# Product rows added by VectorE through a PSUM bank, and the Toeplitz kernel split once, in a gated long-convolution and MoE kernel

## The chip, the cores and the metric

The kernel runs on one core of one Trainium2 chip. A core has TensorE (PE), VectorE (DVE), ScalarE (ACT), GpSimd (POOL) and SyncE (SP, which here only issues DMAs). The metric is the device time of one execution in microseconds (us). Three runs of the kernel before took 830.1, 830.31 and 832.09 us, the median is 830.31.

## The reference

x is (8, 256, 512), the context c the same shape. All is float32.

```python
kv  = einsum('bhil,bhjl->bijhl', c, c)          # 32 heads of 8 channels, L = 512
y   = causal convolution of kv with ssm_kernel[h] along l      # by FFT
out = einsum('bijhl,bhil->bjhl', y + kv * D[h], layernorm(x))
x   = x + tanh(g_xattn) * out
t   = layernorm(x)
x   = x + tanh(g_ffn) * (sum of top-2 of 16 SwiGLU experts, weighted + 2 shared SwiGLU blocks)(t)
```

Per head there are 8 x 8 products kv, of which 36 are distinct, since k and v are the same context. D is added to the kernel's first tap.

## The kernel before, in words

The program has two stages. The first (convolution, residual, layernorm, gate logits, storing of t) works on 16 tiles of 128 rows, one tile a turn. A tile is two heads, each with 8 channels and 8 batches. The second is the expert feed-forward with routing; the change doesn't touch its code.

A turn t of stage one, by engine. Each engine runs its own list of instructions in order and waits on semaphores:

- **SP** issues the loads of tile t+2 (context cx, Toeplitz rows toep, x in xt and xr, a slice `stage` of the shared weights) and the stores of tile t-1 (x2, t, tT), in the order of its `turn`. toep is read from a small table kpad in HBM, whose rows overlap, so that partition p holds the kernel shifted by p.
- **POOL**: `form` multiplies the context into kv, 36 x 64 = 2304 elements a partition, for tile t+1 (L367, L371); then `split_shared` (L1270), `split_toep` (L380) and its part of `split_kv` (L1276). kv has one buffer: `form` of the next tile waits until both parts of kv_lo are made.
- **ACT**: the square root for the second layernorm of tile t-1 (L543), shared_hi (L594), toep_hi (L581), kv_hi (L588), the normalised t (L557), the same for x of tile t+1 (L539, L549), copies of PE's transposes (L567, L568, L574).
- The **hi and lo** parts: PE multiplies in a rounded float32 form, so each operand is a rounded hi and a rest lo = value - hi, and each product is three matmuls (hi hi, hi lo, lo hi).
- **PE**: the turn has four blocks lb = 0..3 of 128 positions. `conv` of block lb has 6(lb+1) matmuls of 288 columns (L1135) in a pair of PSUM banks, for two heads; 60 a turn. `sum_rows` adds seven rows of products with seven accumulating transposes (L1145); it stands behind the next block's `conv`. `gate` (L1115, 8 rows), `turn_t` and `turn_q` (L1095, 4 each) make up the rest.
- **DVE**: `products` of each block multiplies y in PSUM by q, per head with three instructions (L750 256 elements, L753 192, L756 64) into nine rows of 128 in the SBUF tile prod, then one instruction adds two rows to two others (L760, 256 elements, all in SBUF). Between the blocks stand `residual` (L721, behind block 0, with the statistics L697, L699, L700), `scale_x2` and `stats_x` (behind block 1), `scale_x` and DVE's part of kv_lo (L766, 1280 elements, behind block 2).

Engines alternate between two buffers of nearly everything (cx, toep, kv_hi, kv_lo, q, prod, the two pairs of PSUM banks). Turns 3 to 14 are a hardware loop.

Of the kernel before, what the change touches and what calls it, by code (L numbers as in the profile page):

```python
# [146 lines left out]
def program(nc, x, ctx_ext, conv_rows, conv_d, gates, gate_w, weights, out):  # L147
    ctx = ExitStack()
    with ctx:
# [12 lines left out]
        kpad = nc.dram_tensor("kpad", (HEADS, 640), F32, kind="Internal").ap()  # L162
# [3 lines left out]
        toeplitz = bass.AP(kpad.tensor, 0, [[2 * 640, TILES], [1, P], [640, 2], [1, L]])  # L166
# [30 lines left out]
        toep = sb2("toep", [P, 2 * L], F32, one)  # L197
# [76 lines left out]
        toeph_ok, toepl_ok = sem("toeph_ok"), sem("toepl_ok")  # L274
        conv_ok, prod_ok, summed = sem("conv_ok"), sem("prod_ok"), sem("summed")
# [100 lines left out]
        def split_toep(eng, t):  # L376

            p = t.odd
            wait(eng, toeph_ok, t + 1)
            eng.tensor_tensor(toep_lo[p][:], toep[p][:], toep_hi[p][:].bitcast(F32), ALU.subtract).then_inc(toepl_ok, 1)  # L380
# [20 lines left out]
        def _(sp):  # L401
# [79 lines left out]
            sp.wait_ge(toepl_ok, TILES)  # L481
# [49 lines left out]
        def _(act):  # L531
# [44 lines left out]
            def split_toep_hi(t):  # L576

                p = t.odd
                wait(act, conv_ok, (t - 1) * 8)
                wait(act, toep_in[p], (t.half() + 1) * 16)  # L580
                act.activation(toep_hi[p][:], toep[p][:], ACT.Copy).then_inc(toeph_ok, 1)  # L581

# [103 lines left out]
        def _(dve):  # L686
# [5 lines left out]
            dve.tensor_tensor(krow[:, P - 1:P], krow[:, P - 1:P], drow[:], ALU.add).then_inc(kpad_ok, 1)  # L692

# [40 lines left out]
            def products(t, lb):  # L734
# [5 lines left out]
                for h in range(2):  # L740
                    y = ps_conv[par][h][:]
# [37 lines left out]
            split_kv(At(0))  # L779
            split_toep(dve, At(0))  # L780
# [3 lines left out]
            def turn(t):  # L784
# [305 lines left out]
        def _(pe):  # L1090
# [12 lines left out]
            def turn_t(t):  # L1103
                wait(pe, tT_ok, t)
                wait(pe, t_ok, t + 1)
                turn_rows(t1[t.odd], ps_t, t_turned)

            def gate(t):
# [5 lines left out]
                for c in range(BLOCKS):  # L1114
                    last = pe.matmul(ps_gate[:, 0:EXPERTS], tT[t.odd][:, c * P:(c + 1) * P],  # L1115
# [3 lines left out]
            def conv(t, lb):  # L1119
# [3 lines left out]
                for h in range(2):  # L1123
                    if h == 0:
                        if lb == 0:
                            wait(pe, toepl_ok, t + 1)
                            wait(pe, kvl_ok, t + 1)
                            wait(pe, kvl2_ok, t + 1)
                        wait(pe, prod_ok, (t * 4 + lb - 1) * PROD_STEPS)
                    for mb in range(lb + 1):  # L1130
# [3 lines left out]
                        for m, (w, z) in enumerate(((toep_hi, kv_hi), (toep_hi, kv_lo), (toep_lo, kv_hi))):  # L1134
                            mm = pe.matmul(ps_conv[lb % 2][h][:, 0:n], w[p][:, k:k + P], z[p][:, o:o + n],  # L1135
# [3 lines left out]
            def sum_rows(t, lb):  # L1139
# [3 lines left out]
                wait(pe, prod_ok, (t * 4 + lb + 1) * PROD_STEPS)  # L1143
                for r in ROWS_LEFT:
                    mm = pe.matmul(ps_o[:, lb * P:(lb + 1) * P], prod[lb % 2][:, r * P:(r + 1) * P], ident[:],  # L1145
                                   is_transpose=True, start=(r == ROWS_LEFT[0]), stop=(r == ROWS_LEFT[-1]))
# [112 lines left out]
        def _(pool):  # L1259
# [21 lines left out]
            def turn(t):  # L1281
# [118 lines left out]
```

## Time and profile before

| what | value |
|---|---|
| median of the runs | 830.31 us |
| the profiled execution | 832.62 us |
| its span, first to last instruction | 830.8 us |
| mean granted TensorE clock | 0.97 of full |
| stage one, about | 0 to 290 us |
| PE busy | 756.1 us, 91% |
| DVE busy | 657.3 us, 79% |
| ACT busy | 444.6 us, 54% |
| POOL busy | 382.4 us, 46% |
| L760, the add of product rows | x64, 108.3 us |
| L766, DVE's part of kv_lo | x16 |

Busy time is the sum of the records of an engine, and a share over the whole span mixes two stages with different limits. For this change only stage one matters, where a turn starts with the first L750 of the tile's block 0; the turn lengths are differences of such starts.

### The profile page before, as it was taken

The numbers are of one execution on the slowest core, as the hardware profiler recorded it, in microseconds if no ns is written. First come the engines' busy times: TensorE is split into PE (matmuls) and PEld (weight loads), VectorE is DVE, ScalarE is ACT, GpSimd is POOL, SyncE is SP. The second block draws the span as 40 slices with busy tenths as digits, with TensorE's granted clock in tenths as the row PEclk, the third lists the DMA queues.
The fourth block names the chain that finished last, engine by engine and source line by source line (L and its number), as shares of the span: only waits on it lengthen the run. The fifth ranks groups of instructions, "written<-read, shape, count | busy, mean of one in ns | idle before, by whom it ended". The sixth has DMA issues, their size and how long they took to land.

```text
span 830.8 us, 15761 instructions
## 1 busy us (share of the span) xinstructions
PE 756.1 (91%) x4730; PEld 708.6 (85%) x4730; DVE 657.3 (79%) x1167; ACT 444.6 (54%) x594; POOL 382.4 (46%) x206
## 2 busy tenths in 40 slices
PE   3888887787889999999999999989999999999994
PEld 3887787787888889999999999979989989899993
DVE  7999999999999854684258958866986885896891
ACT  5333344343343233221258958766876875895882
POOL 5767657667567001451123443534444344554242
PEclk9999899999889999999999999999999999999997
DMA  6334544334442213121724668767656665443200
GB/s 231 123 122 137 169 153 135 133 121 158 159 141 77 90 64 52 32 45 26 266 51 134 168 168 236 190 197 180 183 168 149 196 170 162 102 80 63 53 14 0
DMA packets 43027, 105.86 MB, mean 127 GB/s; under 512 B 7121, under 2 KB 7121, under 8 KB 42961
## 3 DMA queue, kind: packets, MB, share of 16 engines
q1 hardware_dynamic: 30128, 80.15, 28.4%
q0 software_dynamic: 12832, 24.93, 15.6%
q8 instruction: 30, 0.49, 0.2%
q14 instruction: 37, 0.30, 0.1%
HBM read 148.87 MB, written 29.18 MB: 214 GB/s over the span
## 4 chain that ended last, share of the span: by engine, by line
PE 58%; DVE 24%; issue 7%; DMA 4%; ACT 2%; SPq 1%; ACTq 1%; DVEq 0%; POOL 0%; POOLq 0%
PE bank L1198 29%; PE bank L1223 16%; DVE prod L760 9%; PE bank L1135 5%; DVE prod L750 3%; DVE prod L753 3%; PE bank L1145 3%; PE bank L1206 3%; DMA raw<-in_weights 2%; PE bank L1095 2%; DVE st L697 2%; DMA out<-ys,slot_info 2%; DVE prod L756 1%; DVE kv_lo L766 1%; ACT w_hi L663 1%
## 5 line engine op out<-in xcount | busy, mean ns | idle before, releaser
L1068 DVE TENSOR_TENSOR w_lo<-raw,w_hi 128x1408 fp32r<-128x1408 f32 x94 | 148.8, 1621 | 45.9 <-ACT w_hi L656 45.8
L1334 POOL DMA_INDIRECT out<-ys,slot_info x47 | 87.1, 1853 | 101.0 <-DMA out<-ys,slot_info 58.0
L1323 POOL DMA_INDIRECT tn<-t_rows,slot_info x47 | 71.2, 1516 | 131.9 <-DVE tT_lo L808 120.3
L656 ACT ACTIVATE w_hi<-raw 128x1408 fp32r x94 | 125.0, 1375 | 7.4 <-DMA raw<-in_weights 5.5
L760 DVE TENSOR_TENSOR prod<-prod 128x256 f32<-128x256 f32 x64 | 108.3, 1692 | 0.0
L1135 PE MATMUL bank<-kv_hi,toep_hi 128*128 128x288 f32 x320 | 105.7, 330 | 2.3 <-DVE toep_lo L380 2.3
L1077 DVE TENSOR_TENSOR hid<-hid,bank 128x352 f32<-128x352 f32 x79 | 40.7, 515 | 81.6 <-ACT hid L670 81.6
L1135 PE MATMUL bank<-kv_hi,toep_lo 128*128 128x288 f32 x320 | 100.0, 313 | 0.0
L1135 PE MATMUL bank<-kv_lo,toep_hi 128*128 128x288 f32 x320 | 99.8, 312 | 0.0
L670 ACT ACTIVATE hid<-bank 128x352 f32<-128x352 f32 x79 | 36.0, 456 | 115.9 <-PE bank L1198 115.9
L1073 DVE TENSOR_TENSOR w_lo<-raw,w_hi 128x1536 fp32r<-128x1536 f32 x47 | 82.4, 1752 | 17.6 <-ACT w_hi L663 17.6
L1145 PE MATMUL bank<-ident,prod 128*128 128x128 f32 x448 | 67.7, 296 | 29.5 <-DVE prod L760 29.5
L1198 PE MATMUL bank<-w_hi,tT_hi 128*128 128x352 f32 x376 | 90.9, 323 | 3.4 <-DVE w_lo L1068 3.3
L1198 PE MATMUL bank<-w_hi,tT_lo 128*128 128x352 f32 x376 | 90.7, 322 | 0.0
L1198 PE MATMUL bank<-w_lo,tT_hi 128*128 128x352 f32 x376 | 90.6, 322 | 0.0
L1145 PEld LDWEIGHTS bank<-ident,prod 128*128 128x128 f32 x448 | 56.4, 153 | 32.8 <-DVE prod L760 31.9
L367 POOL TENSOR_TENSOR kv<-cx 128x2048 f32<-128x2048 f32 x15 | 65.4, 4360 | 31.2 <-DVE kv_lo L766 31.2
L663 ACT ACTIVATE w_hi<-raw 128x1536 fp32r x47 | 69.4, 1478 | 15.4 <-DMA raw<-in_weights 15.3
L1198 PEld LDWEIGHTS bank<-w_hi,tT_hi 128*128 128x128 f32 x376 | 66.9, 189 | 8.1 <-issue 4.5
L1135 PEld LDWEIGHTS bank<-kv_hi,toep_hi 128*128 128x128 f32 x320 | 66.0, 206 | 2.7 <-DVE toep_lo L380 2.7
L1334 POOL DMA_INDIRECT out<-ys,own_row x16 | 28.1, 1756 | 83.1 <-ACT ys L644 76.0
L1198 PEld LDWEIGHTS bank<-w_lo,tT_hi 128*128 128x128 f32 x376 | 66.0, 189 | 0.0
(184 smaller groups left out, 1861.0 us busy)
## 6 DMA issues: line engine op xcount, KB each, us to landing
raw<-in_weights SPq DMA_DIRECT2D x94, 704.0 KB
raw<-in_weights SPq DMA_DIRECT2D x47, 768.0 KB
toep<-kpad SPq DMA_DIRECT2D x16, 512.0 KB, 4.5
cx<-in_ctx SPq DMA_DIRECT2D x16, 384.0 KB, 3.2
stage<-in_weights SPq DMA_DIRECT2D x16, 272.0 KB, 2.7
xt<-in_x SPq DMA_DIRECT2D x16, 256.0 KB, 4.5
xr<-in_x SPq DMA_DIRECT2D x16, 256.0 KB, 2.7
out<-x SPq DMA_DIRECT2D x16, 256.0 KB, 2.1
```

The costliest lines, as they stand in the source:

```text
L367: eng.tensor_tensor(view(kv[:], 0, [[PAIRS * BATCH, g], [hb, 4], [1, hb]]), view(cx[p][:], 0, [[EXT * BATCH, g], [0, 4], [1, hb]]), view(c ...
L656: act.activation(w_hi[s % 2][:, a:b], raw[:, bass.ds(half + a, b - a)], ACT.Copy).then_inc(hi_ok[n_], 1)
L663: act.activation(w_hi[s % 2][:, W13:WROW], raw[:, bass.ds(half + W13, W2)], ACT.Copy).then_inc(hi_ok[2], 1)
L760: dve.tensor_tensor(prod[par][:, 5 * P:7 * P], prod[par][:, 0:2 * P], prod[par][:, 5 * P:7 * P], ALU.add).then_inc(prod_ok, 1)
L1068: dve.tensor_tensor(w_lo[s % 2][:, a:b], raw[:, bass.ds(half + a, b - a)], w_hi[s % 2][:, a:b].bitcast(F32), ALU.subtract).then_inc(lo_ok[ ...
L1073: dve.tensor_tensor(w_lo[s % 2][:, W13:WROW], raw[:, bass.ds(half + W13, W2)], w_hi[s % 2][:, W13:WROW].bitcast(F32), ALU.subtract).then_i ...
L1135: mm = pe.matmul(ps_conv[lb % 2][h][:, 0:n], w[p][:, k:k + P], z[p][:, o:o + n], start=(mb == 0 and m == 0), stop=(mb == lb and m == 2))
L1145: mm = pe.matmul(ps_o[:, lb * P:(lb + 1) * P], prod[lb % 2][:, r * P:(r + 1) * P], ident[:], is_transpose=True, start=(r == ROWS_LEFT[0]), ...
L1198: mm = pe.matmul(dst[:, 0:INTER], a[:, c * P:(c + 1) * P], w[:, f:f + INTER], start=(c == 0 and k == 0), stop=(c == BLOCKS - 1 and k == 2))
L1223: mm = pe.matmul(y_bank(u.o)[:], a[:, c * P:(c + 1) * P], w[:, f0 + c * L:f0 + (c + 1) * L], start=(first and c == 0 and k == 0), stop=(la ...
L1323: pool.indirect_dma_start(out=tn[o % 2][:], out_offset=None, in_=t_rows, in_offset=bass.IndirectOffsetOnAxis(ap=slot_info[:, 3 * i:3 * i + ...
L1334: pool.indirect_dma_start(out=out, out_offset=bass.IndirectOffsetOnAxis(ap=rows, axis=0), in_=ys[o % 2][:], in_offset=None, bounds_check=R ...
```

## The change

- **Product rows.** Five rows are kept in prod. The instructions for the other four rows (L753, L756 before) write to a PSUM bank, ps_rows (bank 7). One instruction of 512 elements adds that bank to the first four rows of prod and writes a new SBUF tile `rows`. It waits for all six products; the second product of the next block waits for it. `sum_rows` has five transposes, four of `rows` and one of prod.
- **Bank 7** held the gate logits; they move to the first 16 columns of ps_t (bank 6), and `turn_t` waits for the logits of two tiles before.
- **Toeplitz.** krow (32 x 640) is split once: ACT makes krow_hi, DVE krow_lo, and both go to HBM. Each turn loads toep_hi and toep_lo straight into place. ACT's toep_hi and POOL's toep_lo of each turn go. The loads stand last in SP's turn and wait for the last convolution of the tile that uses the buffer.
- **kv_lo** is all POOL's (2304 elements) but for the first tile.
- The pairs of PSUM banks are declared as one tensor each; the same columns are used.

```diff
-PRODROWS = 9
-ROWS_LEFT = (2, 3, 4, 5, 6, 7, 8)
-PROD_STEPS = 7
+PRODROWS = 5
+PROD_STEPS = 6
...
-            sp.wait_ge(kpad_ok, 1)
-            sp.dma_start(kpad, krow[:]).then_inc(kpad_out, 16)
-            sp.wait_ge(kpad_out, 16)
+            sp.wait_ge(krowh_ok, 1)
+            sp.dma_start(kpad[0], krow_hi[:].bitcast(F32)).then_inc(kpad_out, 16)
+            sp.wait_ge(krowl_ok, 1)
+            sp.dma_start(kpad[1], krow_lo[:].bitcast(F32)).then_inc(kpad_out, 16)
+            sp.wait_ge(kpad_out, 32)
...
-                    wait(sp, toepl_ok, t + 1)
-                    load(t + 2, "toep")
...
+                if ahead:
+                    wait(sp, conv_ok, (t + 1) * 8)
+                    load(t + 2, "toep")
...
-                    split_toep_hi(t + 1)
...
-                    split_kv(t + 1)
...
-                    split_toep(pool, t + 1)
...
-                    dve.tensor_tensor(view(pp, po + 5 * P, [[P, 3], [G, HD], [1, BATCH]]),
+                    if h == 0:
+                        wait(dve, rows_ok, t * 4 + lb)
+                    dve.tensor_tensor(view(ps_rows, po, [[P, 3], [G, HD], [1, BATCH]]),
...
-                    dve.tensor_tensor(view(pp, po + 8 * P, [[4 * G, 2], [G, 4], [1, BATCH]]),
+                    dve.tensor_tensor(view(ps_rows, po + 3 * P, [[4 * G, 2], [G, 4], [1, BATCH]]),
...
-                wait(dve, prod_ok, (t * 4 + lb) * PROD_STEPS + 5)
-                dve.tensor_tensor(prod[par][:, 5 * P:7 * P], prod[par][:, 0:2 * P], prod[par][:, 5 * P:7 * P],
-                                  ALU.add).then_inc(prod_ok, 1)
+                wait(dve, prod_ok, (t * 4 + lb + 1) * PROD_STEPS)
+                dve.tensor_tensor(rows[par][:], ps_rows, prod[par][:, 0:L], ALU.add).then_inc(rows_ok, 1)
...
-                wait(pe, prod_ok, (t * 4 + lb + 1) * PROD_STEPS)
-                for r in ROWS_LEFT:
+                wait(pe, rows_ok, t * 4 + lb + 1)
+                for r in range(PRODROWS):
+                    part = (rows if r < BLOCKS else prod)[lb % 2]
...
-                pool.tensor_tensor(kv_lo[t.odd][:, KV_DVE:], kv[:, KV_DVE:], kv_hi[t.odd][:, KV_DVE:].bitcast(F32),
+                a = KV_DVE if t.within(0, 1) else 0
+                pool.tensor_tensor(kv_lo[t.odd][:, a:], kv[:, a:], kv_hi[t.odd][:, a:].bitcast(F32),
```

DVE's list at block 0 of turn 1, before (prod is SBUF, bank and pair are PSUM):

```order
L750 TENSOR_TENSOR prod<-bank,q 128x4x8x8 [waits conv_ok,q_ok,summed]
L753 TENSOR_TENSOR prod<-bank,q 128x24x8
L756 TENSOR_TENSOR prod<-bank,q 128x8x8
L750 TENSOR_TENSOR prod<-bank,q 128x4x8x8 [waits conv_ok]
L753 TENSOR_TENSOR prod<-bank,q 128x24x8
L756 TENSOR_TENSOR prod<-bank,q 128x8x8
L760 TENSOR_TENSOR prod<-prod 128x256 [waits prod_ok]
L721 SCALAR_TENSOR_TENSOR x<-bank,small,xr 128x512 [waits summed,xr_in0]
```

The same place now:

```order
L746 TENSOR_TENSOR prod<-pair,q 128x4x8x8 [waits conv_ok,q_ok,summed]
L751 TENSOR_TENSOR bank<-pair,q 128x24x8 [waits rows_ok]
L754 TENSOR_TENSOR bank<-pair,q 128x8x8
L746 TENSOR_TENSOR prod<-pair,q 128x4x8x8 [waits conv_ok]
L751 TENSOR_TENSOR bank<-pair,q 128x24x8
L754 TENSOR_TENSOR bank<-pair,q 128x8x8
L758 TENSOR_TENSOR rows<-bank,prod 128x512 [waits prod_ok]
L717 SCALAR_TENSOR_TENSOR x<-bank,small,xr 128x512 [waits summed,xr_in0]
```

The number of instructions is the same; four of them write to PSUM, and the add has one operand in PSUM and twice the elements.

POOL's list for one turn, before, from the multiplication into kv to the next one:

```order
L367 TENSOR_TENSOR kv<-cx 128x8x256 [waits ctx_in0,kvl2_ok,kvl_ok]
L371 TENSOR_TENSOR kv<-cx 128x8x32
L1270 TENSOR_TENSOR shared_lo<-stage,shared_hi 128x544 [waits shi_ok]
L380 TENSOR_TENSOR toep_lo<-toep,toep_hi 128x1024 [waits toeph_ok]
L1276 TENSOR_TENSOR kv_lo<-kv,kv_hi 128x1024 [waits kvh_ok]
```

and now:

```order
L370 TENSOR_TENSOR kv<-cx 128x8x256 [waits ctx_in0,kvl2_ok]
L374 TENSOR_TENSOR kv<-cx 128x8x32
L1268 TENSOR_TENSOR shared_lo<-stage,shared_hi 128x544 [waits shi_ok]
L1275 TENSOR_TENSOR kv_lo<-kv,kv_hi 128x2304 [waits kvh_ok]
```

toep_lo is gone, kv_lo is whole, and `form` no longer waits for DVE (kvl_ok).

SP's list for turn 0, the loads of tile 2, before:

```order
L420 DMA cx<-in_ctx 128x768 [waits kv_ok]
L417 DMA toep<-kpad 128x2x512 [waits toepl_ok]
L422 DMA xt<-in_x 128x512 [waits xn_ok]
L426 DMA stage<-in_weights 128x544 [waits slo_ok]
```

and now:

```order
L420 DMA cx<-in_ctx 128x768 [waits kv_ok]
L422 DMA xt<-in_x 128x512 [waits xn_ok]
L426 DMA stage<-in_weights 128x544 [waits slo_ok]
L417 DMA toep_hi<-kpad_hi 128x2x512 [waits conv_ok]
L417 DMA toep_lo<-kpad_lo 128x2x512
```

Two loads stand where one stood, and they are behind the turn's other loads (and, from turn 1 on, its three stores).

## Rows read from the trace of the kernel before

**Rows 1.** The page, part 2: DVE and bytes moved, 40 slices of 20.8 us.

```profile
DVE  7999999999999854684258958866986885896891
GB/s 231 123 122 137 169 153 135 133 121 158 159 141 77 90 64 52 32 45 26 266 51 134 168 168 236 190 197 180 183 168 149 196 170 162 102 80 63 53 14 0
```

**Rows 2.** Starts of turns 1 and 15, DVE timeline: start, duration in us.

```profile
31.86 0.41 DVE L750 TENSOR_TENSOR prod<-bank,q 128x256 f32<-128x256 f32 x1
...
274.37 0.41 DVE L750 TENSOR_TENSOR prod<-bank,q 128x256 f32<-128x256 f32 x1
```

**Rows 3.** Fourteen turns: length, busy of PE, PEld, DVE, ACT, POOL, clock, DMA share, GB/s.

```profile
31.86:274.37 242.51, 203.41 (x1448) 195.02 (x1448) 239.36 (x575) 96.36 (x140) 155.62 (x69) 0.92 0.40 133
```

**Rows 4.** Lines of DVE: duration in ns, min/median/max, and starts.

```profile
L760 DVE TENSOR_TENSOR prod<-prod x64: 403/1246/3397, 16.8 to 285.8; 128x256 f32<-128x256 f32 x64
...
L750 DVE TENSOR_TENSOR prod<-bank,q x128: 390/414/426, 15.3 to 285.0; 128x256 f32<-128x256 f32 x128
...
L766 DVE TENSOR_TENSOR kv_lo<-kv,kv_hi x16: 1479/1481/2028, 10.9 to 271.2; 128x1280 fp32r<-128x1280 f32 x16
```

**Rows 5.** The page, part 5: busy us, mean ns of one, idle before.

```profile
L760 DVE TENSOR_TENSOR prod<-prod 128x256 f32<-128x256 f32 x64 | 108.3, 1692 | 0.0
```

**Rows 6.** Timeline of DVE and POOL around the start of a turn at 189.41.

```profile
184.91 4.29 POOL L367 TENSOR_TENSOR kv<-cx 128x2048 f32<-128x2048 f32 x1 [2.08 <-DVE kv_lo L766]
...
186.21 3.28 DVE L760 TENSOR_TENSOR prod<-prod 128x256 f32<-128x256 f32 x1
...
189.16 0.92 POOL L371 TENSOR_TENSOR kv<-cx 128x256 f32<-128x256 f32 x1
189.41 0.41 DVE L750 TENSOR_TENSOR prod<-bank,q 128x256 f32<-128x256 f32 x1
...
190.14 0.41 DVE L750 TENSOR_TENSOR prod<-bank,q 128x256 f32<-128x256 f32 x1
...
190.74 0.20 DVE L756 TENSOR_TENSOR prod<-bank,q 128x64 f32<-128x64 f32 x1
...
190.87 0.41 DVE L760 TENSOR_TENSOR prod<-prod 128x256 f32<-128x256 f32 x1
...
191.20 0.73 DVE L721 SCALAR_TENSOR_TENSOR x<-bank,small,xr 128x512 f32<-128x512 f32 x1
```

**Rows 7.** Timeline of ACT in the same turn.

```profile
192.97 0.29 ACT L543 ACTIVATE sd<-mv,small 128x1 f32<-128x1 f32 x1 [6.52 <-DVE mv L700]
...
193.72 1.05 ACT L581 ACTIVATE toep_hi<-toep 128x1024 fp32r<-128x1024 f32 x1
...
194.68 2.11 ACT L588 ACTIVATE kv_hi<-kv 128x2304 fp32r<-128x2304 f32 x1
```

**Rows 8.** Lines of POOL, duration in ns, min/median/max.

```profile
L1276 POOL TENSOR_TENSOR kv_lo<-kv,kv_hi x16: 2354/2402/2417, 9.2 to 268.3; 128x1024 fp32r<-128x1024 f32 x16
...
L1270 POOL TENSOR_TENSOR shared_lo<-stage,shared_hi x16: 1348/1366/1374, 19.0 to 279.1; 128x544 f32 x12, 128x544 fp32r<-128x544 f32 x4
...
L380 POOL TENSOR_TENSOR toep_lo<-toep,toep_hi x15: 2577/2589/2597, 20.4 to 265.7; 128x1024 fp32r<-128x1024 f32 x15
```

**Rows 9.** The chain of waits, PE's pieces: start, us, and matmuls.

```profile
190.63 2.88 PE bank L1135 x12
193.51 0.91 PE bank L1145 x7
194.43 2.39 PE bank L1135 x18
```

**Rows 10.** Timeline of PE: the gate's eight rows.

```profile
186.60 1.04 PE L1115 MATMUL bank<-gw,tT 128*128 128x16 f32 x8
```

**Rows 11.** The page, part 6: KB of one load, median us from issue to landing.

```profile
toep<-kpad SPq DMA_DIRECT2D x16, 512.0 KB, 4.5
```

**Rows 12.** Timeline of the start: DVE's first multiplication into kv, POOL's first kv_lo.

```profile
4.34 2.27 DVE L367 TENSOR_TENSOR kv<-cx 128x2048 f32<-128x2048 f32 x1
...
9.19 2.35 POOL L1276 TENSOR_TENSOR kv_lo<-kv,kv_hi 128x1024 fp32r<-128x1024 f32 x1 [7.46 <-ACT kv_hi L588]
```

More of the change, by code:

```diff
@@ L170, in program @@
         out_t = out.rearrange("(t p) l -> t p l", p=P)
-        bank = [ctx.enter_context(nc.psum_tensor(f"bank{n}", [P, 512], F32)) for n in range(8)]
-        ps_conv = [[bank[0], bank[1]], [bank[2], bank[3]]]
-        ps_o, ps_q, ps_t, ps_gate = bank[4], bank[5], bank[6], bank[7]
+        ps_conv = [ctx.enter_context(nc.psum_tensor(f"pair{n}", [P, 1024], F32)) for n in range(2)]
+        bank = [ps_conv[n // 2][:, n % 2 * 512:n % 2 * 512 + 512] for n in range(4)]
+        bank += [ctx.enter_context(nc.psum_tensor(f"bank{n}", [P, 512], F32))[:] for n in range(4, 8)]
+        ps_o, ps_q, ps_t, ps_rows = bank[4], bank[5], bank[6], bank[7]
         ps_h, ps_ht, ps_y = [[bank[0], bank[1]], [bank[4], bank[5]]], bank[2], [bank[3], bank[7]]
+        ps_gate = ps_t[:, 0:EXPERTS]
         ps_rank, ps_total, ps_table = bank[4], bank[5], bank[7]
@@ L196, in program @@
         cx = sb2("cx", [P, BLOCKS * GROUPS * EXT], F32, one)
-        toep = sb2("toep", [P, 2 * L], F32, one)
+        xt = sb2("xt", [P, L], F32, one)
+        xn = sb2("xn", [P, L], F32, one)
         stage = sb2("stage", [P, STAGE], F32, one)
@@ L208, in program @@
         kv_lo = sb2("kv_lo", [P, BLOCKS * GROUPS * PAIRS], F32R, one)
-        xt = sb2("xt", [P, L], F32, one)
         xr = sb2("xr", [P, L], F32, one)
-        xn = sb2("xn", [P, L], F32, one)
         q = sb2("q", [P, BLOCKS * GROUPS * EXT], F32, one)
         prod = sb2("prod", [P, PRODROWS * P], F32, one)
+        rows = sb2("rows", [P, L], F32, one)
         krow = sb("krow", [HEADS, 640], F32, one)
+        krow_hi, krow_lo = sb("krow_hi", [HEADS, 640], F32R, one), sb("krow_lo", [HEADS, 640], F32R, one)
         drow = sb("drow", [HEADS, 1], F32, one)
@@ L362, in form @@
             p = t.odd
-            wait(eng, kvl_ok, t)
             wait(eng, kvl2_ok, t)
+            if t.within(1, 2):
+                eng.wait_ge(kvl_ok, 1)
             wait(eng, ctx_in[p], (t.half() + 1) * 16)
@@ L374, in form @@
                               ALU.mult).then_inc(kv_ok, 1)
[L376 to L380, printed above, removed]
         def h_bank(n):
@@ L416, in load @@
                 if which == "toep":
-                    sp.dma_start(toep[p][:].rearrange("p (h c) -> p h c", h=2),
-                                 toeplitz[bass.ds(t.v, 1)].rearrange("x p h c -> (x p) h c")).then_inc(toep_in[p], 16)
+                    for part, rows in ((toep_hi, toeplitz[0]), (toep_lo, toeplitz[1])):
+                        sp.dma_start(part[p][:].bitcast(F32).rearrange("p (h c) -> p h c", h=2),
+                                     rows[bass.ds(t.v, 1)].rearrange("x p h c -> (x p) h c")).then_inc(toep_in[p], 16)
                 if which == "ctx":
@@ L480, in _ @@
             sp.wait_ge(kv_ok, 2 * TILES)
-            sp.wait_ge(toepl_ok, TILES)
+            sp.wait_ge(xn_ok, TILES)
             for p in (0, 1):
@@ L574, in tT_copy @@
                 act.activation(tT[t.odd][:], ps_t[:], ACT.Copy).then_inc(tT_ok, 1)
[L576 to L581, printed above, removed]
             def split_kv_hi(t):
@@ L594, in split_shared @@
                 act.activation(shared_hi[:, bass.ds(t.v * STAGE, STAGE)], stage[p][:], ACT.Copy).then_inc(shi_ok, 1)
+            act.wait_ge(kpad_ok, 1)
+            act.activation(krow_hi[:], krow[:], ACT.Copy).then_inc(krowh_ok, 1)
             split_kv_hi(At(0))
@@ L1105, in turn_t @@
                 wait(pe, t_ok, t + 1)
+                wait(pe, logits_ok, t)
                 turn_rows(t1[t.odd], ps_t, t_turned)
@@ L1114, in gate @@
                 for c in range(BLOCKS):
-                    last = pe.matmul(ps_gate[:, 0:EXPERTS], tT[t.odd][:, c * P:(c + 1) * P],
+                    last = pe.matmul(ps_gate, tT[t.odd][:, c * P:(c + 1) * P],
                                      gw[:, c * EXPERTS:(c + 1) * EXPERTS], start=(c == 0), stop=(c == BLOCKS - 1))
@@ L1125, in conv @@
                         if lb == 0:
-                            wait(pe, toepl_ok, t + 1)
-                            wait(pe, kvl_ok, t + 1)
+                            wait(pe, toep_in[p], (t.half() + 1) * 32)
+                            if t.within(0, 1):
+                                pe.wait_ge(kvl_ok, 1)
                             wait(pe, kvl2_ok, t + 1)
@@ L1142, in sum_rows @@
                     wait(pe, x2_ok, t)
[L1143 to L1146 removed]
+                wait(pe, rows_ok, t * 4 + lb + 1)
+                for r in range(PRODROWS):
+                    part = (rows if r < BLOCKS else prod)[lb % 2]
+                    mm = pe.matmul(ps_o[:, lb * P:(lb + 1) * P], part[:, r * P:(r + 1) * P], ident[:],
+                                   is_transpose=True, start=(r == 0), stop=(r == PRODROWS - 1))
                 mm.then_inc(summed, 1)
```

28 lines of the change are left out of this document (13 added, 15 removed).

## The prediction, made before the changed kernel was run

> **What bounds the kernel now.** I read the page's slices first: DVE is at 9 tenths in every slice but the first up to about 290 us, and falls to 4 to 8 behind it [rows 1]. So stage one is where DVE sets the pace, and the change touches only stage one. Then the turns: the block 0 of turn 1 starts at 31.86, that of turn 15 at 274.37 [rows 2], so 14 turns take 242.51 us, 17.32 us each. DVE is busy 239.36 of these 242.51 us, PE 203.41, POOL 155.62, ACT 96.36 [rows 3]. Nothing else is near DVE.
>
> Then DVE's lines. L760, the add of two rows, has 256 elements and takes 0.403 us at best, 1.692 us on average and 3.397 at worst, with no idle time before it [rows 4, 5]. The products of the same 256 elements take 0.390 to 0.426, all 128 of them [rows 4]. The difference is in the operands: L760 has both in SBUF, the products have one in PSUM. The timeline shows what it pays for: the add that starts at 186.21 lasts 3.28 us and ends at 189.49, just after POOL's instruction of 184.91 to 189.20, and 0.3 us into POOL's next; the add at 190.87, with no POOL instruction beside it, takes 0.41 [rows 6]. So an SBUF-with-SBUF instruction of DVE stands until POOL's running one ends, and 4 adds a turn stand 1.28 us each on average. That is 5.1 of 17.32 us.
>
> **The change, part by part.** Everything is worked out for one turn of the 14.
>
> *DVE.* Gone: four adds at a pitch of their mean less the 0.08 us by which a successor overlaps (0.41 long, next one 0.33 later [rows 6]), 4 x 1.61 = 6.45 us; and the 1280 elements of kv_lo, 1.48 less 0.08 = 1.40 [rows 4]. Come: four adds of 512. From 64 elements at 0.20 to 256 at 0.41 [rows 6] an element costs 1.09 ns, so 512 take 0.41 + 0.28 = 0.69, pitch 0.61. The new add waits for the sixth product, which it followed by 0.13 before; now it must wait for that one's 0.20 and a semaphore, some 0.05, so 0.12 more. 4 x 0.73 = 2.9. DVE's turn becomes 17.32 - 6.45 - 1.40 + 2.9 = 12.4 us.
>
> The trace has no DVE instruction that writes to PSUM, of which there are now 16 a turn. From below the price is 0 (writing as to SBUF; I see no gain in it); from above I take one semaphore-free pass again as long as the shortest product, 0.20 us each, 3.2 us a turn. I take 0, since reading PSUM costs a product nothing that shows against an SBUF add of the same size (0.414 median against 0.403 to 0.41) [rows 4, 6].
>
> That row can be put beside a rule. The Trainium skill, "VectorE: DVE Perf Modes", section "The TRN2 errata", gives VectorE 58 cycles and the elements for an SBUF source and 120 and the elements for a PSUM source at 0.96 GHz, which would make the new add dearer by 62 cycles, an estimate of 0.065 us, or 0.26 us a turn of DVE. The trace does not agree: 0.414 and 0.403 to 0.41 at 256 elements. By the page DVE's turn would be 12.7 us instead of 12.4.
>
> *PE.* 60 matmuls and 28 + 8 transposes become 60 and 20 + 8. At the full clock the pitch is 2.39 / 18 = 0.133 us for matmuls and 0.91 / 7 = 0.13 for transposes [rows 9], the gate is 1.04 [rows 10]. 88 x 0.133 + 1.04 = 12.7 us, 1.0 less than before. At the low clock (2.88 / 12 = 0.24 us a matmul [rows 9]) it is nearly twice that. The 14 turns had 0.92 of the clock, with PE idle for 39 us in them [rows 3].
>
> *POOL.* toep_lo (2.59) goes, kv_lo grows from 1024 to 2304 elements. 1024 take 2.40 and 544 of shared_lo 1.37 [rows 8], so 2.15 ns an element and 5.2 us for 2304. The bounds are 4.8 (at the rate of kv, 4.29 for 2048 [rows 6]) and 5.8 (at toep_lo's rate, 2.59 for 1024 [rows 8]). POOL's turn is 4.29 + 0.92 + 1.37 + 5.2 = 11.8 us of work [rows 6, 8], and it no longer waits about 2.1 us for DVE's part of kv_lo before `form` [rows 6].
>
> *ACT* loses toep_hi, 1.05 us, which stood before kv_hi [rows 7].
>
> *The new loop.* DVE, PE and POOL all come to 12 to 13 us, so what decides is the chain that runs through them once a turn. From the start of a turn: seven instructions to the end of block 0. Before, the second half came 0.73 behind the first and its small product 0.60 behind that [rows 6]; that one's 0.20 and 0.05 bring the add to 1.58, and `residual` to 2.19. From `residual` to ACT's square root it was 192.97 - 191.20 = 1.77 [rows 6, 7]: 3.96. From there past shared_hi to the next ACT instruction 0.75 [rows 7]: 4.71, where now kv_hi stands. Its 2.11 us [rows 7] and a hop of 0.1 (POOL's first kv_lo shows such a release by kv_hi [rows 12]): 6.9. kv_lo, 5.2: 12.1. Then PE's three first matmuls of the next tile and their way into PSUM, an estimate of 0.7 from 3 x 0.133 and a fill of 0.3: 12.8 us, and the next turn starts.
>
> PE arrives at the same place with 82 matmuls and transposes and the gate behind it, 82 x 0.133 + 1.04 = 11.95 at the full clock, against kv_lo's 12.1. That is no cover at all, so each late start of one of them adds. I add 0.6 us a turn for it: 13.4 us. 14 x (17.32 - 13.4) = 54.9 us gained.
>
> *SP and the loads.* toep doubles from 512 KB a turn [rows 11] and stands last, behind the store of tT, which waits for ACT's last instruction of the turn. So it is issued some 0.3 us into the next turn, and needed about 12 us later. 512 KB took 4.5 us to land [rows 11]; twice that, 9 us, fits. The wait for the convolution (about 10 us into the turn) is over by then and holds nothing up; cx and xt of the next turn stand behind two loads instead of one, about 0.5 us, and are needed some 6 us and more later. Cost 0. With the cover gone (a turn below about 10 us) they would be the bound.
>
> *Start.* DVE's first multiplication into kv started at 4.34 [rows 12]. It now stands behind krow_lo, which waits for ACT, whose table load ends late: by 640 elements on each, about 2.7 us later. Two small stores instead of one and 1 MB before the first convolution: POOL's chain for tile 1, kv, kv_hi, kv_lo, starts at 15.8 instead of 13 to 14, but no longer stalls. I get turn 1 at about 30 instead of 31.86, 2 us gained, with 2 us either way. The last turn and the hand-over I count at 0 (the adds were short there already), the gate in another bank at 0: what it waits for is two turns old.
>
> *Sum.* The profiled execution took 832.62 us (span 830.8), 2.3 above the median of the runs. 832.6 - 54.9 - 2 = 775.7; against the median 773.4.
>
> **The rivals.**
>
> *The clock falls.* Were the granted clock to stay at 0.92 as before [rows 3], PE's 12.7 would be 13.8, and with its waits a turn of 14.3 us: 786. For it: PE waits for DVE, ACT and POOL in each turn. Against it: it would be busy for 95% of a turn, 84% before. 0.17.
>
> *Writing to PSUM is dear.* At 0.13 us each, 16 of them, DVE's turn is 14.5 and the turn 14.7 us: 792. No row speaks for or against. 0.08.
>
> *Everything fits better.* kv_lo at 4.8 and no slack: a turn of 12.4 us, 759. For it: the instructions' times scatter by a few per cent at most [rows 4, 8]. 0.17.
>
> *The add is held up by POOL all the same*, because one operand and the result are in SBUF. Then the turn is 17.32 - 1.40 + 4 x (0.28 + 0.12) = 17.5 us: 14 x 0.2 = 2.8 us lost and 2 gained, 831, no change. Against it: the products have the same kind of operands and never took over 0.426 us [rows 4]. 0.03.
>
> *The loads become the bound, and the kernel is slower.* A turn moves 133 GB/s x 17.32 us = 2.3 MB [rows 3]; with another 0.52 MB it is 2.8. Slower than before it is from the point where the queue can't give 2.8 MB / 17.32 us = 163 GB/s to this pattern. If it stays at 133, a turn takes 21.2 us: 832.6 + 14 x 3.9 - 2 - 2.3, 883 against the median. For it: the slices of stage one behind the first lie between 121 and 169 GB/s [rows 1]; at 13.4 us a turn 211 would be wanted. Against it: the first slice had 231 with the same kind of loads, another 266 [rows 1], and the DMA share was 0.40 [rows 3]. 0.03.
>
> **How the numbers follow.** The forecast, turns of 12.8 to 13.9 us and 765 to 780 us, has 0.52. The range is 757 to 791: it takes in the clock, the better fit, and the PSUM writes up to 0.13 us each; beyond it lie 0.06 of the last two and a little of the rest. A change within 0.3% (2.5 us) is what a measurement of this kernel can't tell from none: that is the held-up add, 0.03. Slower by more: the loads, 0.03. Faster: 0.94.
>
> **What would show it.** The new add at 0.65 to 0.75 us, all 64 of them, with no long ones beside POOL. The products that write to PSUM at 0.34 and 0.21 as before. Turns (first product of block 0 to the next) of 13.4 us; DVE busy for about 92% of them, PE 95% at a clock near 1. PE's wait before the first matmul of a tile ended by POOL's kv_lo of about 5.2 us. Loads of toep that end well before. The forecast is wrong if turns are above 14.5 or below 12.3 us, if PE waits there for a DMA, or if stage two changes its length by more than 2 us.

## The result and the profile after

The changed kernel took 769.04 us (median of 4 runs, 767.48 to 771.24) against 830.96 for the kernel before (4 runs, 830.1 to 832.09): a ratio of 0.9256, with a 95% interval of 0.9229 to 0.9283. The forecast was 773.4 us in 757 to 791.

The profiled execution has a span of 767.5 us, 63.3 less. Four pieces of it, each a difference of starts in the two traces: the start of turn 1 moved from 31.86 to 30.49 (1.4 us); the 14 turns from there to turn 15 take 181.52 us instead of 242.51 (61.0), so 12.97 us each instead of 17.32; from turn 15 to the last residual it is 13.54 instead of 13.82 (0.3); and all that follows 541.95 instead of 542.61 (0.7). That last piece is stage two, whose code is untouched; it differs by some us from one execution to the next (e7 below), so the 0.7 says nothing.

The page of the changed kernel, part 2 (DVE, the granted clock, bytes moved, 40 slices of 19.2 us):

```profile
DVE  5889898999975469433799588679758985895892
...
PEclk9999999999999999999999999999999999999998
...
GB/s 194 224 188 246 226 238 236 229 246 218 207 96 70 56 28 42 42 242 74 129 173 178 116 256 182 176 188 197 176 112 179 139 210 149 94 73 72 42 16 0
```

The same columns as [rows 3], for the changed kernel's 14 turns:

```profile
30.49:212.01 181.52, 175.36 (x1338) 165.36 (x1337) 165.62 (x560) 84.05 (x126) 160.86 (x56) 1.00 0.70 224
```

DVE was busy for 99% of the turns and is at 91%. PE went from 84 to 97%, POOL from 64 to 89%, the clock from 0.92 to 1.00, the DMA traffic from 133 to 224 GB/s. PE, DVE and POOL are now within 8 points of each other, as forecast.

The lines that answer to [rows 4], durations in ns, min/median/max (L758 is the new add, L746 the product that still goes to SBUF, L751 and L754 write to PSUM):

```profile
L758 DVE TENSOR_TENSOR rows<-bank,prod x64: 691/692/694, 18.8 to 223.1; 128x512 f32<-128x512 f32 x64
...
L746 DVE TENSOR_TENSOR prod<-pair,q x128: 390/416/425, 17.2 to 222.2; 128x256 f32<-128x256 f32 x128
...
L751 DVE TENSOR_TENSOR bank<-pair,q x128: 353/356/361, 17.5 to 222.6; 128x192 f32<-128x192 f32 x128
...
L754 DVE TENSOR_TENSOR bank<-pair,q x128: 221/224/228, 17.8 to 222.8; 128x64 f32<-128x64 f32 x128
```

and the same two products in the kernel before, where they wrote to SBUF:

```profile
L753 DVE TENSOR_TENSOR prod<-bank,q x128: 336/346/357, 15.6 to 285.4; 128x192 f32<-128x192 f32 x128
...
L756 DVE TENSOR_TENSOR prod<-bank,q x128: 204/211/216, 15.9 to 285.6; 128x64 f32<-128x64 f32 x128
```

The add with twice the elements takes 692 ns, all 64 within 3 ns, where the old one had 403 to 3397. Writing to PSUM costs 10 and 13 ns an instruction, 0.18 us a turn.

The chain that was forecast as the new bound, in the turn that starts at 108.20. DVE, ACT, POOL and PE timelines of the changed kernel:

```profile
108.20 0.42 DVE L746 TENSOR_TENSOR prod<-pair,q 128x256 f32<-128x256 f32 x1 [0.79 <-PE pair L1132]
...
110.40 0.74 DVE L717 SCALAR_TENSOR_TENSOR x<-bank,small,xr 128x512 f32<-128x512 f32 x1
```

```profile
112.19 0.29 ACT L544 ACTIVATE sd<-mv,small 128x1 f32<-128x1 f32 x1 [3.94 <-DVE mv L696]
112.39 0.65 ACT L588 ACTIVATE shared_hi<-stage 128x544 f32 x1
112.95 2.12 ACT L582 ACTIVATE kv_hi<-kv 128x2304 fp32r<-128x2304 f32 x1
```

```profile
111.86 0.74 POOL L374 TENSOR_TENSOR kv<-cx 128x256 f32<-128x256 f32 x1
113.24 1.37 POOL L1268 TENSOR_TENSOR shared_lo<-stage,shared_hi 128x544 f32 x1 [0.65 <-ACT shared_hi L588]
115.14 5.14 POOL L1275 TENSOR_TENSOR kv_lo<-kv,kv_hi 128x2304 fp32r<-128x2304 f32 x1 [0.53 <-ACT kv_hi L582]
```

```profile
119.19 0.66 PE L1090 MATMUL bank<-ident,xn 128*128 128x128 f32 x4 [0.21 <-ACT xn L550]
...
120.11 0.27 PE L1143 MATMUL bank<-ident,prod 128*128 128x128 f32 x1
120.52 0.40 PE L1132 MATMUL pair<-kv_hi,toep_hi 128*128 128x288 f32 x1
```

Measured from the turn's start, with the forecast in brackets: residual 2.20 (2.19), square root 3.99 (3.96), kv_hi 4.75 (4.71), kv_lo 6.94 (6.9), its end 12.08 (12.1), and the next turn 12.97 (12.8). PE's last transpose starts at 120.11, and the first matmul of the next tile at 120.52, behind kv_lo's end at 120.28. In all 14 turns it starts 0.10 to 0.27 us behind kv_lo's end. Where it waits for nothing, as in e9 below, its row starts 0.03 behind the transpose's. So PE came 0.38 us early (the expectations below count 0.28, with a step of 0.13).

### The profile page after: what moved, and what is told of

Its sections match the earlier page's. It is cut to its first block, busy times and chain, and to the rows that moved or that the text cites. A ratio compares the mean times of both kernels' runs of the same rounds, so it can differ in the third digit from the quotient of the medians.

```text
span 767.5 us, 15537 instructions
## 1 busy us (share of the span) xinstructions
PE 725.1 (94%) x4602; PEld 675.8 (88%) x4602; DVE 577.8 (75%) x1152; ACT 431.1 (56%) x579; POOL 381.5 (50%) x191
## 4 chain that ended last, share of the span: by engine, by line
PE 58%; DVE 16%; DMA 8%; issue 7%; ACT 5%; SPq 2%; ACTq 1%; DVEq 1%; POOL 0%; POOLq 0%
PE pair L1196 15%; PE bank L1196 12%; PE pair L1221 10%; PE bank L1221 5%; PE pair L1132 5%; DMA out<-ys,slot_info 4%; DMA raw<-in_weights 3%; PE bank L1090 3%; PE bank L1143 3%; PE pair L1204 2%; DVE st L693 2%; DVE prod L746 2%; DVE bank L751 2%; DVE rows L758 2%; ACT xn L550 2%
## 5 line engine op out<-in xcount | busy, mean ns | idle before, releaser
L1132 PE MATMUL pair<-kv_hi,toep_hi 128*128 128x288 f32 x320 | 100.5, 314 | 4.4 <-issue 1.9
L1132 PE MATMUL pair<-kv_hi,toep_lo 128*128 128x288 f32 x320 | 95.3, 298 | 0.0
L1132 PE MATMUL pair<-kv_lo,toep_hi 128*128 128x288 f32 x320 | 95.1, 297 | 0.0
L1275 POOL TENSOR_TENSOR kv_lo<-kv,kv_hi 128x2304 fp32r<-128x2304 f32 (+1 forms) x16 | 79.6, 4972 | 18.8 <-ACT kv_hi L582 18.8
L1132 PEld LDWEIGHTS pair<-kv_hi,toep_hi 128*128 128x128 f32 x320 | 61.1, 191 | 8.2 <-issue 6.6
L746 DVE TENSOR_TENSOR prod<-pair,q 128x256 f32<-128x256 f32 x128 | 53.1, 415 | 16.5 <-PE pair L1132 16.5
L1132 PEld LDWEIGHTS pair<-kv_lo,toep_hi 128*128 128x128 f32 x320 | 61.1, 191 | 0.0
L1132 PEld LDWEIGHTS pair<-kv_hi,toep_lo 128*128 128x128 f32 x320 | 60.9, 190 | 0.0
L1196 PE MATMUL pair<-w_hi,tT_hi 128*128 128x352 f32 x192 | 46.0, 321 | 0.5 <-DVE w_lo L1063 0.5
L1196 PE MATMUL pair<-w_hi,tT_lo 128*128 128x352 f32 x192 | 46.0, 321 | 0.0
```

The lines of the kernel that those rows point to most:

```text
L746: dve.tensor_tensor(view(pp, po, [[P + G, 4], [G, HD], [1, BATCH]]), view(y, 0, [[HB, 4], [BATCH, HD], [1, BATCH]]), view(qq, qo, [[0, 4], ...
L1132: mm = pe.matmul(ps_conv[lb % 2][:, h * 512:h * 512 + n], w[p][:, k:k + P], z[p][:, o:o + n], start=(mb == 0 and m == 0), stop=(mb == lb a ...
L1196: mm = pe.matmul(dst[:, 0:INTER], a[:, c * P:(c + 1) * P], w[:, f:f + INTER], start=(c == 0 and k == 0), stop=(c == BLOCKS - 1 and k == 2))
L1275: pool.tensor_tensor(kv_lo[t.odd][:, a:], kv[:, a:], kv_hi[t.odd][:, a:].bitcast(F32), ALU.subtract).then_inc(kvl2_ok, 1)
```

## The experiments

Turns are the mean of 14, from the first product of turn 1 to that of turn 15, read from each run's trace. The turn is in us, and so is the mean of the add. e1 to e7 have one time each, e8 to e12 five or six (the median is given).

| run | us | turn 1 at | a turn | the add, mean |
|---|---|---|---|---|
| before | 830.96 | 31.86 | 17.32 | 1.69 |
| changed | 769.04 | 30.49 | 12.97 | 0.69 |
| e1 add in SBUF | 829.97 | 34.19 | 17.14 | 1.92 |
| e2 rows only | 788.84 | 28.84 | 14.57 | 0.69 |
| e3 rest only | 827.94 | 33.98 | 16.92 | 1.78 |
| e4 seven transposes | 776.11 | 32.27 | 12.99 | 0.69 |
| e5 kv_hi first | 778.06 | 29.80 | 13.69 | 0.69 |
| e6 sum first | 769.22 | 29.91 | 12.96 | 0.69 |
| e7 loads twice | 775.62 | 36.44 | 13.16 | 0.69 |
| e8 both orders | 778.93 | 29.32 | 13.69 | 0.69 |
| e9 shared_hi ahead | 765.90 | 30.18 | 12.67 | 0.69 |
| e10 e9, e6 and early load | 764.69 | 29.08 | 12.82 | 0.69 |
| e11 changed again | 769.53 | 29.98 | 12.97 | 0.69 |
| e12 e9 and early load | 763.09 | 29.16 | 12.67 | 0.69 |

### Is it the PSUM operand?

**e1**, the same instructions with the bank replaced by an SBUF tile `more`:

```diff
-                    dve.tensor_tensor(view(ps_rows, po, [[P, 3], ...
+                    dve.tensor_tensor(view(more[:], po, [[P, 3], ...
...
-                dve.tensor_tensor(rows[par][:], ps_rows, prod[par][:, 0:L], ALU.add)
+                dve.tensor_tensor(rows[par][:], more[:], prod[par][:, 0:L], ALU.add)
```

> The changed kernel, but the four rows that went to the PSUM bank go to a tile of the same size in SBUF, so the 512-element add has both operands in SBUF. Theory (the add is held while POOL works whenever both its operands are in SBUF): adds from 0.69 us at best to 3 to 5 us, mean about 2 us, turns of 17 to 18 us, 820 to 840 us in all. Rival (the gain comes from fewer instructions and rows, and DVE's kv_lo gone): adds of 0.69 us and 766 to 773 us, as the changed kernel.

829.97 us: 61 us are gone again by the place of one tile, which four products of each block write and the add reads. The add's line, and one add of DVE beside POOL's kv_lo:

```profile
L759 DVE TENSOR_TENSOR rows<-more,prod x64: 691/1400/3571, 18.3 to 285.9; 128x512 f32<-128x512 f32 x64
```

```profile
164.78 3.02 DVE L759 TENSOR_TENSOR rows<-more,prod 128x512 f32<-128x512 f32 x1
```

```profile
162.11 5.14 POOL L1276 TENSOR_TENSOR kv_lo<-kv,kv_hi 128x2304 fp32r<-128x2304 f32 x1 [0.54 <-ACT kv_hi L583]
```

The best add takes 691 ns as with PSUM; the one at 164.78 ends at 167.80, 0.55 us behind POOL's at 167.25. So it is held until POOL's instruction is over, and then does most of its own 0.69 us. The traces show the same of every add. In e1, 46 of the 64 start while an instruction of POOL runs, and each ends 0.54 to 0.56 us behind that instruction's end; the other 18 take 0.691 to 0.693. In the kernel before, 46 end 0.28 to 0.29 behind POOL's end, and the other 18 take 0.403 to 0.412. So in both the end comes by the add's own time, less some 0.13 us, behind POOL's, whatever POOL is running (kv, kv_lo, shared_lo). The theory holds; fewer transposes and the loss of DVE's kv_lo alone take a turn from 17.32 to 17.14 only.

**e2**, the kernel before with only the product rows changed; **e3**, the changed kernel with only the product rows as before (the parts of the diff ahead of the prediction are taken whole; the add stands for them here).

```diff
 # e2: on the kernel before
+                wait(dve, prod_ok, (t * 4 + lb + 1) * PROD_STEPS)
+                dve.tensor_tensor(rows[par][:], ps_rows, prod[par][:, 0:L], ALU.add).then_inc(rows_ok, 1)
 # e3: on the changed kernel
+                dve.tensor_tensor(prod[par][:, 5 * P:7 * P], prod[par][:, 0:2 * P], prod[par][:, 5 * P:7 * P],
+                                  ALU.add).then_inc(prod_ok, 1)
```

> The kernel before with the product rows of the change alone (PSUM bank, add of 512, five transposes); toep is split each turn and DVE keeps its 1280 elements of kv_lo. Theory (the held adds were the greater part): turns of 13.8 to 14.5 us, DVE bound, since its kv_lo of 1.4 us stays and can be held by POOL, 783 to 797 us. Rival (both parts are needed, as toep and kv_lo on POOL and ACT hold the turn): turns above 16 us, over 810 us.

> The changed kernel with the product rows of the kernel before (nine rows in SBUF, add of 256 in SBUF, seven transposes); Toeplitz split once, kv_lo all on POOL. Theory (a busier POOL holds the adds longer, which eats what DVE gains by giving up 1.4 us): adds of 1.9 to 2.3 us on average, turns of 16.5 to 17.5 us, 815 to 835 us. Rival (the parts add up): adds as long as before, 1.69 us, turns of 15.9 us, 808 to 813 us.

The rows alone take a turn from 17.32 to 14.57 us (a little above the range), the rest alone to 16.92. Together it is 12.97, so the rest is worth 0.41 us a turn without the rows and 1.60 with them. The reason is in these two lines, DVE's kv_lo in e2 and the add in e3:

```profile
L769 DVE TENSOR_TENSOR kv_lo<-kv,kv_hi x16: 2201/2550/2627, 10.8 to 228.1; 128x1280 fp32r<-128x1280 f32 x16
```

```profile
L756 DVE TENSOR_TENSOR prod<-prod x64: 406/1250/3545, 18.4 to 282.4; 128x256 f32<-128x256 f32 x64
```

In e2 the one large DVE instruction left in the turns with both operands in SBUF takes 2.55 us instead of 1.48 [rows 4]; it is now the one that is held, and all 16 end 1.35 us behind an instruction of POOL. DVE is still the bound there: it is busy for 199.27 of the 203.93 us of the 14 turns. In e3 held adds last up to 3.5 us, 1.78 on average. I had expected 1.9 to 2.3; the total, 827.94, was in the range.

### What sets the new turn?

**e4**, two more transposes in each sum (their sums are other ones, so its routing differs and its total can't be compared; the turn can):

```diff
-                for r in range(PRODROWS):
+                picks = (0, 1, 2, 3, 4, 4, 4)
+                for k, r in enumerate(picks):
...
```

> The changed kernel with seven transposes in each sum of rows instead of five (the fifth row is added three times, so the sums are other ones). Eight more a turn, 1.06 us of PE. If PE's own work sets the turn of 12.97 us: 14.0 us, 784 us. If the chain through xn, turn_q and the sum behind it sets it: two of the eight lie in it, 13.2 us a turn, 773 us. If only the chain through kv_lo does: 12.97 us, 769 us.

12.99 us a turn: eight more transposes cost 0.02. PE and POOL timelines of e4:

```profile
122.28 0.49 PE L1144 MATMUL bank<-ident,prod 128*128 128x128 f32 x3
122.70 0.40 PE L1132 MATMUL pair<-kv_hi,toep_hi 128*128 128x288 f32 x1
```

```profile
117.31 5.15 POOL L1276 TENSOR_TENSOR kv_lo<-kv,kv_hi 128x2304 fp32r<-128x2304 f32 x1 [0.53 <-ACT kv_hi L582]
```

kv_lo ends at 122.46, 0.24 before the matmul, as before. The two transposes that lie ahead of it (two steps more, 0.22 us) have taken PE's lead from 0.38 to 0.17 us (the last of the three starts at 122.50, the matmul at 122.70, less the step of 0.03). So the turn was set by the chain to kv_lo.

The expectation of 14.0 for a turn bound by PE rested on a count of 12.7 us that is itself too large. Three transposes in 0.49 us, one of them 0.27, are 0.11 us a step and not 0.13, and the eight rows of the gate are 0.11 us a step too. PE's work in a turn of the changed kernel is then 60 x 0.133 + 28 x 0.11 + 8 x 0.11 = 11.9 us, and the rest are waits: 0.38 for kv_lo, 0.38 for xn (119.19 above) and 0.28 for the add of block 1 (at 114.59). The eight transposes of e4 are 0.9 us and fill these waits; with 12.8 us of work PE is just short of being the bound there.

**e5**, ACT's and POOL's order turned:

```diff
-                split_shared(t)
                 if not t.within(TILES - 1, TILES):
                     split_kv_hi(t + 1)
+                split_shared(t)
... (POOL)
-                split_shared(t)
                 if not t.within(TILES - 1, TILES):
                     split_kv(t + 1)
+                split_shared(t)
```

> The changed kernel, with kv_hi ahead of shared_hi on ACT and kv_lo ahead of shared_lo on POOL; nothing is added or left out. Theory (the chain residual, square root, shared_hi, kv_hi, kv_lo, first matmul sets the turn of 12.97 us, and the chain through xn is 0.28 us behind it): kv_lo is ready 0.54 us earlier, the turn falls by the 0.28 to 12.69, about 765 us. Rival (PE's own work sets it): 12.97 us, 769 us.

Both theories missed: 13.69 us a turn, 778.06 us. POOL's timeline of e5 shows a third one:

```profile
98.68 4.34 POOL L370 TENSOR_TENSOR kv<-cx 128x2048 f32<-128x2048 f32 x1
102.97 0.75 POOL L374 TENSOR_TENSOR kv<-cx 128x256 f32<-128x256 f32 x1
105.96 5.14 POOL L1275 TENSOR_TENSOR kv_lo<-kv,kv_hi 128x2304 fp32r<-128x2304 f32 x1 [2.24 <-ACT kv_hi L582]
111.06 1.35 POOL L1268 TENSOR_TENSOR shared_lo<-stage,shared_hi 128x544 f32 x1
112.37 4.34 POOL L370 TENSOR_TENSOR kv<-cx 128x2048 f32<-128x2048 f32 x1
```

kv has one buffer, so POOL's own round is kv, wait for ACT's kv_hi, kv_lo, and again. From these rows, start to start: 4.29 + 0.75 + 2.24 + 5.10 + 1.31 = 13.69. In the changed kernel shared_lo stood in the wait for kv_hi; here it stands behind kv_lo, and POOL idles 2.24 us. The order that I took for a detour on the chain was POOL's filling.

**e6**, PE's sum of block 2 ahead of xn's transposes; **e8**, e5 and e6 and the context of tile 1 loaded first.

```diff
+                sum_rows(t, 2)
                 if not last:
                     turn_q(t + 1)
-                sum_rows(t, 2)
```

> The changed kernel, with PE's sum of the rows of block 2 ahead of the transposes of xn; nothing is added or left out. This shortens the chain through xn by 0.55 us and leaves that through kv_lo. Theory (kv_lo sets the turn): 12.97 us, 769 us. Rival (xn's chain sets it): 12.6 to 12.7 us, 764 us.

> The changed kernel with both orders of the two runs before (kv_hi and kv_lo first, sum of block 2 before xn's transposes), and the load of the context of tile 1 issued before the split krow, as POOL waited 2.4 us for it. Theory: both chains are 0.5 us shorter, PE's own work of 12.6 to 12.7 us is what is left, and turn 1 starts 1 to 2 us earlier: 762 to 765 us. Rival (the turn is at PE's work already, 12.97): 767 to 768 us, from the start alone.

e6: 12.96 us, 769.22 us. The chain through xn does not set the turn. e8 was expected at 762 to 765 and took 778.93 us (ratio 0.9366, 0.9333 to 0.9400), 13.69 us a turn: POOL's round again, as it was sent with e5 and shares its flaw.

**e7**, each toep load twice.

```diff
+                        sp.dma_start(spare[...][p][:]..., rows[bass.ds(t.v, 1)]...).then_inc(toep_in[p], 16)
...
-                            wait(pe, toep_in[p], (t.half() + 1) * 32)
+                            wait(pe, toep_in[p], (t.half() + 1) * 64)
```

> The changed kernel, with each toep load issued twice (the second copy goes to spare tiles, and PE waits for both), 1 MB more a turn, some 3.9 MB in all. Theory (the loads have room): turns of 13.0 to 13.4 us, 769 to 776 us, at about 300 GB/s. Rival (the queue gives no more than the 240 GB/s seen so far in a slice): turns of 16 us, 812 us.

Turns 13.16 us, 775.62 us: 5.9 us more in the start (turn 1 at 36.44), 2.7 in the 14 turns. The time behind the last residual was 539.5 us there against 541.95; it was 545.3 in e9's profile and 541.9 in e12's, so stage two differs by some us from one execution to the next, which is why the turns and not the totals tell the mechanisms apart. A stretch of e7's turns, columns as in [rows 3]:

```profile
60.00:200.00 140.00, 133.63 (x1024) 126.17 (x1023) 125.65 (x425) 63.79 (x97) 122.71 (x44) 1.00 0.99 311
```

The queues give 311 GB/s at a busy share of 0.99, and the turns scatter there from 12.91 to 13.52. The changed kernel's 224 GB/s at 0.70 have room; by these rates it would end at turns of about 9.3 us (12.97 x 224 / 311), an estimate.

### A shorter chain that keeps POOL's filling

**e9**, shared_hi ahead of the square root on ACT, POOL's order as it was; **e10**, that with e6 and the early load; **e11**, the changed kernel on the same chip; **e12**, e9 with the early load.

```diff
+                split_shared(t)
                 if not t.within(0, 1):
                     std_x2(t - 1)
-                split_shared(t)
 # early load, e10 and e12
+            sp.dma_start(cx[1][:], ctx_ext[1]).then_inc(ctx_in[1], 16)
             sp.wait_ge(krowh_ok, 1)
...
-            load(At(1), "ctx")
```

> The changed kernel, with shared_hi ahead of the square root of the second layernorm on ACT; POOL's order stays. kv_hi then follows the square root at once, and POOL's shared_lo still fills the time of kv_hi. Theory (the chain to kv_lo sets the turn; in the order with kv_hi first it was POOL's own round, with shared_lo no longer beside kv_hi): kv_lo ready 0.4 us earlier, the xn chain 0.28 us behind decides, turns of 12.7 us, 765 us. Rival (any change of this order costs a wait elsewhere, as there): 12.97 us or more, 769 us or more.

> As the run before, and also PE's sum of block 2 ahead of xn's transposes and the context of tile 1 loaded before the split krow. Theory: both chains shorter, POOL's round of 12.55 us and PE's own 12.6 to 12.7 are left; turns of 12.65 us and a start 0.5 to 1.5 us earlier, 762 to 764 us. Rival: 12.97 us a turn, 768 us.

> The changed kernel as it is, on the same chip as the two runs before, for comparison: 769 us, turns of 12.97 us.

> The changed kernel with shared_hi ahead of the square root, as in the run that gave turns of 12.67 us, and the context of tile 1 loaded before the split krow, with PE's order left alone. Theory (PE's sum ahead of xn's transposes cost 0.15 us a turn, since it delays the copies of q; the early load gives about 1 us): turns of 12.67 us, turn 1 at about 29.1 us, 764 to 765 us. Rival (the early load delays toep by as much): 766 us as without it.

e9: 12.67 us a turn, 765.90 us, ratio to before 0.9199 (0.9173 to 0.9226), e11 0.9245 (0.9219 to 0.9272). The intervals of the totals touch; the turns, 12.67 against 12.97, do not. kv_hi now follows the square root at once (ACT and POOL timelines of e9):

```profile
110.14 0.29 ACT L544 ACTIVATE sd<-mv,small 128x1 f32<-128x1 f32 x1 [3.09 <-DVE mv L696]
110.34 2.12 ACT L582 ACTIVATE kv_hi<-kv 128x2304 fp32r<-128x2304 f32 x1
```

```profile
110.24 1.38 POOL L1268 TENSOR_TENSOR shared_lo<-stage,shared_hi 128x544 f32 x1
112.54 5.16 POOL L1275 TENSOR_TENSOR kv_lo<-kv,kv_hi 128x2304 fp32r<-128x2304 f32 x1 [0.92 <-ACT kv_hi L582]
```

What sets the turn of e9 is another loop. PE no longer waits for kv_lo: its first matmul follows the last transpose at once, 0.03 behind, in the last 12 of the 14 turns (PE timeline):

```profile
105.38 0.27 PE L1143 MATMUL bank<-ident,prod 128*128 128x128 f32 x1
105.41 0.38 PE L1132 MATMUL pair<-kv_hi,toep_hi 128*128 128x288 f32 x1
```

The chain of waits of e9 runs from the residual through DVE's list to xn, then through PE's transposes, ACT's copies of q and tT, PE's gate and the sum of block 3 back to the residual:

```profile
105.90 0.61 ACT tT L575
...
106.56 1.06 PE bank L1111 x8
```

POOL's own round is close below it, 12.52 us from one kv (105.25) to the next (117.77).

e10 was no shorter but longer than e9, 12.82 us a turn. The chain of waits of e10 names what it hit (start, length):

```profile
104.44 0.45 PE bank L1090 x4
...
105.67 0.61 ACT tT L575
...
106.33 1.06 PE bank L1111 x8
```

xn's transposes stand behind the five of the sum, 0.5 us, ACT copies q and only then tT, and PE's gate waits for tT, with a sum and the next convolution behind it: the loop that sets e9's turn has got longer. e12 leaves this out: 12.67 us a turn, turn 1 at 29.16, 763.09 us (762.39 to 764.05), ratio 0.9181 (0.9154 to 0.9208). It beats both kernels, the changed one by about 6 us.

## Why the prediction was right

- **DVE bound by adds that POOL holds.** Shown: the adds of the changed kernel take 692 ns, and e1 gives the 61 us up again by putting that operand in SBUF. One reading was a little off: DVE's slices stand at 9 up to about 270 us, and at 8 from there to 290 [rows 1]. The rival in which the add is held up all the same is out.
- **DVE's turn of 12.4 us.** Its busy time is 165.62 / 14 = 11.8 us; the rest of a turn it waits, for PE above all. The add was priced at 0.69 and is 0.692.
- **PSUM writes at 0.** 0.010 to 0.013 us each; 16 of them 0.18 us a turn. The upper bound of 0.20 each was far off. The other step, that a PSUM source costs nothing, stands for the product (0.416 against 0.403 for the old add at its best). The rule of the Trainium skill ("VectorE: DVE Perf Modes", section "The TRN2 errata"), 62 cycles more for a PSUM source, does not agree with these runs: the 512-element adds of e1 and of the changed kernel, alike but for one operand's place, take 691 ns at best.
- **The new loop.** The chain was right piece by piece to 0.04 us up to kv_lo's end; only the last piece, from there to the next turn, was 0.9 instead of 0.7. That kv_lo ends PE's wait is shown by e4 and e6, where PE and xn's chain move and the matmul stays 0.10 to 0.27 us behind kv_lo's end.
- **The 0.6 us for late starts** was the term that was too large: 12.97 instead of 13.4, 14 x 0.43 = 6.0 us. The profiled execution, forecast at 775.7, took 769.46, so this term is nearly all of the miss; the start gained 0.6 less than forecast, and the last tile and stage two 1.0 more. The turns scatter by 0.15 us (12.90 to 13.05) and nothing adds up, since the clock stayed at 1.00. I had argued there was no cover, since PE would arrive at 11.95 against kv_lo's 12.1. That count was the error: at 0.11 us a step for the transposes and the gate, PE's work to that place is 54 x 0.133 + 28 x 0.11 + 8 x 0.11 = 11.1 us. It could wait 0.66 us for other engines on its way and still come 0.38 early. So of the 0.6 only 0.17 was needed, and the miss is a size, not the mechanism. The rival of a falling clock is out by the same row.
- **POOL's kv_lo**, 5.2, is 5.15. **POOL's round** I counted as 11.8 us of work, without the wait for kv_hi inside it; with it the round is 12.5 us (e9), close below the chain. That omission did no harm here and is why e5 and e8 missed.
- **Loads.** Landing medians 4.1 and 6.0 us for toep_hi and toep_lo instead of 4.5 for one; issued 0.6 to 0.8 us into most turns, not 0.3. e7 shows the room. The 121 to 169 GB/s that I read for stage one leave out its last slices, with 77 and 90 [rows 1]; the rival of the loads doesn't hang on them.
- **Start** 30.49, forecast about 30. DVE's first kv began at 7.36, 3.0 us later; POOL's first one started at 16.94, having waited 2.4 us for its context; with the early load (e12) it starts at 15.89, and what it waits for then is DVE's part of the first kv_lo, which ends at 15.75.

## What to carry to other kernels

A VectorE instruction with two SBUF operands beside a busy GpSimd can cost many times its own work; look for one whose shortest and longest rows are far apart and whose end stands at a fixed distance behind an end of GpSimd's, and move one operand to PSUM. When the bound goes, add up the chain that runs once round the loop through all engines, and apart from it each engine's own round with the waits inside it. An instruction that seems to stand in the way on one engine may be what fills another's wait.

## What was not expected of the hardware

- The DMA traffic of this pattern, loads and stores, reached 311 GB/s over 140 us (e7).
- A write to PSUM is dearer for VectorE than to SBUF, but by 10 to 13 ns an instruction only.
- The hold goes the other way too, but only for the end of it. GpSimd's small multiplication into kv (256 elements) took 0.92 us in the kernel before [rows 6] and in e3, where a held add of 0.41 us ends 0.28 behind the instruction before it, 1.18 in e1, where that tail is 0.55, and 0.73 in e2 and the changed kernel, where no held add ends there. So a GpSimd instruction that follows at once is longer by the tail less some 0.1 us. toep_lo shows it as well: 2.59 [rows 8], and 2.41 in e2. The large multiplication follows kv_lo 0.18 us later and is longer by that much less: 4.63 in e1 against 4.34, and hardly at all in e3 (4.36). That it takes 4.29 in the kernel before and 4.34 in the changed one, no run explains. The lines of POOL in e1 and in the changed kernel:

```profile
L375 POOL TENSOR_TENSOR kv<-cx x15: 1167/1179/1204, 20.4 to 258.1; 128x256 f32<-128x256 f32 x15
```

```profile
L374 POOL TENSOR_TENSOR kv<-cx x15: 724/735/747, 21.2 to 202.4; 128x256 f32<-128x256 f32 x15
```
